# A Mamba, attention and gated feed-forward layer in two passes: two adding transfers, one accumulation and one transposition of the first pass moved one step

## The reference, cut to what matters

```
xc, res = x @ W_in.T                          # 1024 channels each
u     = silu(conv4(xc) + b_conv)
dt, B, C = u @ W_xproj.T                      # 32, 16 and 16 columns
delta = softplus(dt @ W_dt.T + b_dt)
h[t]  = exp(delta[t] * A) * h[t-1] + delta[t] * B[t] * u[t]     # 16 states per channel
y[t]  = sum over the 16 states of h[t] * C[t]
out   = ((y + u * D) * silu(res)) @ W_out.T
x     = layernorm(x + out)
```

## Time and profile before

| what | value |
|---|---|
| runs | 2470.24 and 2456.21 us, median 2463.22 us |
| profiled execution | 2475.47 us, its span 2473.7 us |
| first pass in it | about 1,700 us of the span |
| PE busy, whole span | 2333.5 us (94%) |
| DVE busy, whole span | 1852.8 us (75%) |
| ACT busy, whole span | 1565.1 us (63%) |
| POOL busy, whole span | 1670.3 us (68%) |
| granted clock of TensorE, mean | 0.981 |

### The profile page before, as it was taken

One profiled execution on the slowest core, in us unless ns is written; L12 is line 12 of the kernel. 1 busy time (PEld: TensorE's weight loads), 2 busy tenths in 40 slices (PEclk: granted clock), 3 DMA queues, 4 the chain that ended last, 5 costly groups with the idle time before them and its releaser, 6 DMA issues. The chain is left out here.

```text
span 2473.7 us, 38405 instructions
## 1 busy us (share of the span) xinstructions
PE 2333.5 (94%) x15232; PEld 1392.6 (56%) x15232; DVE 1852.8 (75%) x2166; ACT 1565.1 (63%) x2604; POOL 1670.3 (68%) x909
## 2 busy tenths in 40 slices
PE   8898999999899999999999999898899999999998
PEld 4565666566566666556666655554545554554553
DVE  4998898898899899889889887772474565466363
ACT  3786887878778788777788877762333343443432
POOL 1898899898899889888989888882432333233130
PEclk9999999999999999999999999998899999999999
DMA  6677978877877878797787777866200100000000
GB/s 207 141 154 161 223 156 177 218 169 164 212 163 171 189 191 168 158 225 160 174 216 164 175 185 180 196 148 170 103 1 34 35 18 18 34 18 1 17 18 17
DMA packets 103525, 329.57 MB, mean 133 GB/s; under 512 B 9571, under 2 KB 46819, under 8 KB 72627
## 3 DMA queue, kind: packets, MB, share of 16 engines
q0 software_dynamic: 27648, 201.34, 41.3%
q1 hardware_dynamic: 75699, 125.78, 14.9%
HBM read 107.25 MB, written 18.51 MB: 51 GB/s over the span
## 5 line engine op out<-in xcount | busy, mean ns | idle before, releaser
L1020 POOL TENSOR_TENSOR mamba_ring<-mamba_ring,mamba_c_row 128x1024 f32<-128x1024 f32 x512 | 1277.0, 2655 | 45.1 <-DVE mamba_ring L908 44.6
L908 DVE TENSOR_TENSOR_SCAN mamba_ring<-mamba_ring,ps 128x512 f32<-128x512 f32 x1024 | 1175.0, 1201 | 141.1 <-PE ps L452 135.7
L713 ACT ACTIVATE mamba_ring<-mamba_delta,mamba_a_neg 128x512 f32<-128x512 f32 x1024 | 660.4, 710 | 91.6 <-DMA mamba_ring<-mamba_ring 90.0
L452 PEld LDWEIGHTS ps<-shared,mamba_v_t 64*128 64x128 f32 x8192 | 501.2, 189 | 257.8 <-issue 148.0
L452 PE MATMUL ps<-shared,mamba_v_t 64*128 64x128 f32 x8192 | 583.4, 285 | 62.1 <-DVE mamba_ring L908 61.0
L1029 POOL DMA_DIRECT2D mamba_ring<-mamba_ring x192 | 181.5, 945 | 154.9 <-DMA mamba_ring<-mamba_ring 130.5
L1703 POOL TENSOR_TENSOR xf_pr<-xf_pr,xf_top 128x1232 f32<-128x1232 f32 x32 | 75.0, 2343 | 255.5 <-DVE xf_top L1602 255.5
L418 PE MATMUL ps<-mamba_xt,mamba_wres 128*128 128x512 f32 x512 | 242.1, 616 | 0.0
L361 PE MATMUL ps<-mamba_xt,mamba_wu 128*128 128x512 f32 x464 | 218.5, 614 | 5.4 <-DMA mamba_xt<-x_t 5.4
L882 DVE SCALAR_TENSOR_TENSOR mamba_u<-ps,mamba_wcv,mamba_u 128x511 f32<-128x511 f32 (+2 forms) x192 | 142.2, 741 | 73.7 <-ACT mamba_u L678 71.2
L504 PE MATMUL ps<-mamba_wout,mamba_u 128*128 128x512 f32 x352 | 167.9, 611 | 0.0
(11 more groups left out here) (150 smaller groups left out, 2859.6 us busy)
## 6 DMA issues: line engine op xcount, KB each, us to landing
mamba_ring<-mamba_ring POOLq DMA_DIRECT2D x192, 1024.0 KB, 7.7
mamba_c_row<-c_rows SPq DMA_DIRECT2D x32, 1024.0 KB, 12.1
mamba_wres<-w_res SPq DMA_DIRECT2D x64, 256.0 KB, 6.5
mamba_wu<-w_u SPq DMA_DIRECT2D x58, 256.0 KB, 4.1
x_rows<-x SPq DMA_DIRECT2D x32, 256.0 KB, 7.5
mamba_xt<-x_t SPq DMA_DIRECT2D x7, 1024.0 KB, 10.7
x<-x_rows SPq DMA_DIRECT2D x28, 256.0 KB, 5.3
xf_xn<-x SPq DMA_DIRECT2D x16, 256.0 KB, 7.8
```

The source lines that it names most:

```text
L452: m = nc.tensor.matmul(ps[:, 2 * s + i, tb * P:(tb + 1) * P], v_t[g % 2][i * H:(i + 1) * H, tb * P:(tb + 1) * P], diag_b[i * H:(i + 1) * H ...
L713: a = nc.scalar.activation(ring[:, q % NR, i, :], delta[:, d % EARLY, :], ACT.Exp, scale=a_neg[:, d, 2 * k + i:2 * k + i + 1])
L908: m = nc.vector.tensor_tensor_scan(ring[:, r, i, :], ring[:, r, i, :], both[:, bass.ds(i, T, 2)], 0.0, ALU.mult, ALU.add)
L1020: nc.gpsimd.tensor_tensor(ring[:, q % NR], ring[:, q % NR], c_row[:, 2 * k:2 * k + 2, :], ALU.mult).then_inc(c_done, 1)
```

## The change

Four things of the first pass move, each to a neighbouring place of the same step list.

- POOL issues the second adding transfer of a group after the product of step 5, and no longer after that of step 6.
- POOL issues the third one after the product of step 0 of the next group, and no longer after that of step 1.
- PE sums the last two slots (`state_sum`) in step 5 and no longer in step 6, and transposes y back in step 6 and no longer in step 7. In step 5 the sum now stands behind the order of step 4, ahead of other products of step 5. The `if` lines of `v_transposes` and `state_sum` have changed places so that they stand in the order of k.
- ACT copies the sum out and writes the skip term in step 6 and no longer in step 7, ahead of all else of that step.

The amount of work, its shapes and its data are the same. The first adding transfer stays where it was, after the product of step 3.

```
@@ -557,11 +557,11 @@  PE
-                if k == 6 and g >= 1:
+                if k == 4 and g + 1 < NG:
+                    v_transposes(g + 1)
+                if k == 5 and g >= 1:
                     for e in SUMS:
                         state_sum(g - 1, e)
-                if k == 4 and g + 1 < NG:
-                    v_transposes(g + 1)
@@ -622,7 +622,7 @@  PE
-                if k == 7 and g >= 1:
+                if k == 6 and g >= 1:
                     y_transposes(g - 1)
@@ -1039,9 +1039,9 @@  POOL
-                    if k == 1 and g >= 1:
+                    if k == 0 and g >= 1:
                         merge(g - 1, 2)
-                    if k in (3, 6):
+                    if k in (3, 5):
                         merge(g, k // 4)
```

## The result

The changed kernel took 2577.57 and 2590.41 us, a median of 2584 us against 2463 us before: +121 us, a ratio of 1.048 with a 95% interval of 1.045 to 1.052. I had forecast slower, 2553 us. The profiled execution took 2577.57 us (span 2575.7), 102 us more than the one of before; +90 us had been forecast for that pair. The second pass kept its length: from the last gating of y to the end there are 762.8 us, and 764.4 before.

The account below looks back on a forecast made before the run. POOL, running behind DVE nearly always, was taken to lead. Longer cycle 153, less 5 (second transfers leaving sooner), 38 (spacing) and 20 (waits for scans), gave +90 us on 2463: 2553 us, range 2500 to 2616 us.

Parts of the forecast that it names:

- POOL's longer cycle: First pass, POOL: each group's cycle grows by one product, 2.43 us, +153 us over 63 distances; +90 us after reliefs.
- Relief by spacing: First transfers, issued longer after a third one, share the DMA engines less: 0.6 us per group, -38 us, bounds 0 and -76.
- rival D: Block 7, DVE: no relief comes and `make_diag` stalls in every batch row, 6.8 us each in three more: +173 us; chance 0.06.
- PE's and ACT's moves at nothing: PE's sum and transposition back, ACT's copy and skip term: costed at 0, at most 28 us of PE freed.
- POOL's waits for scans "vanish": POOL's products before DVE's scans: waits vanish as far as POOL always runs behind, -20 us, bounds 0 and -34.8.
- POOL's unrelieved cycle: First pass, POOL: one product more per group with no relief, +153 us, 2616 us, the range's upper end.
- The rival that the Trainium skill's fit stood behind: POOL's first transfer lands within 5.8 us, so no wait arises, or something else leads: -28 us, 2435 us; chance 0.10.

Follow-up runs that it names:

- the half transfer: First adding transfer of each group adds one of its two slots: on POOL's part alone 2430.7 us, 0.987; on the kernel before 2436.3 us, 0.989.

## Why the prediction was right, and where it was not

**POOL's longer cycle: right for POOL's part by itself.** Forecast +90 us; measured alone +86 us, with the distance from one first transfer to the next up by 1.23 us (1.43 forecast). Its steps one by one: the second transfer can't leave before the first has landed (192 landings of 6.9 us or more; the half transfer shows the point, at 4.5 us the cost is gone). In the changed kernel the product reappears between third and first (+2.77 us of distance, 2.43 forecast; the group shown adds waits for scans). The second to third distance keeps its 9.55 us. Relief by spacing was mis-sized: first transfers land 1.06 us sooner on average, and 0.79 in POOL's part alone; forecast 0.6.

**A term left out.** I kept the stalls of DVE's tiles (rival D) out of the sum, on the ground that POOL's standstill opens gaps for them. In the changed kernel the first tile of block 7 takes 4.3 to 8.5 us in all 7 batch rows that make one; before, it took over 6 us in 4 of them and 0.7 us in the other 3; the 14 tiles take 51.8 us in place of 35.3. That is +16.5 us, where D had 20, and +35 us in POOL's part alone. So the agreement of 90 with 86 is in part luck.

**The failed step: PE's and ACT's moves at nothing.** I wrote that the sum "goes up past one set of `b_products`" and costed PE's move at 0, looking only at what the sum waits for. What counts is what waits behind it. Step 5 has another job on PE, and step 6 has none, so the move stacks 2.0 us on a stretch that already held a job, and the scan of step 7 pays: 13.8 us per batch row in the changed kernel, where all distances between scans together gain 14.8. By itself this part costs 4.3%, more than POOL's, with block 7's wait for the third transfer in it. The forecast put its possible effect between 0 and a gain of 28 us; its sign was wrong.

**POOL's waits for scans "vanish": wrong**, 34.8 to 75.0 us, for the same reason: scans that come late behind PE make POOL wait.

**How the two add.** 3.6% and 4.3% alone give 4.8% together, not 7.9%. On top of PE's and ACT's part, POOL's part costs only 0.5% (1.043 to 1.048, with intervals that overlap), so in the changed kernel PE's part accounts for most of the time. The waits show it: in PE's part alone POOL idles 157.8 us for scans, and its longer cycle fits into that. In POOL's part alone ACT's decays wait 161.8 us for transfers; in the changed kernel 6.5 us, so that POOL's lag hardly reaches the scans by this way. What POOL's part changes on top lies in block 7, and the two halves of it nearly cancel. The third transfer comes early enough for the sum: from scan 6 to scan 7 there are 5.85 us and no longer 12.12, and PE's wait for transfers falls from 44.4 to 12.4 us. And DVE's first tile is stalled again: from scan 1 to scan 2 there are 8.60 us and no longer 3.75, and the 14 tiles take 51.8 us and no longer 18.7. This is read from rows; no run held either fixed.

**The clock** was not in the forecast. The changed kernel has 24 stretches at the lower level; with the sum alone there are 22 and with POOL's part alone 13. No experiment held the clock fixed, so its share stays open. The two distances in blocks 1 and 5 grew by 4.9 us per batch row, 34 us over the 7 batch rows that prepare a next one; that is an estimate of the most that the stretches there cost, as PE's waits before them are in it. What the one in block 7 costs is not in it.

**The range** held the time since its upper end had been set by POOL's unrelieved cycle, +153 us; the middle was low by the second cause. That the whole came within 31 us of the forecast is partly luck: the cause that I named costs about as much alone as I said, but in the changed kernel another one sets most of the time, and the two overlap. Of the rivals none came true as a whole. The rival that the Trainium skill's fit stood behind ("DMA: Bandwidth & Descriptors", anatomy of one DMA) did not: these adding transfers of 1 MB never landed in the 4.4 us that it gives.

## What to carry to other kernels

A step that is moved to "sooner" must be asked two things: does what it waits for come sooner too, and what is queued behind it in its new place? Here a transfer could not leave before another had landed, so an engine idled where it used to work, and a job of 2 us joined a stretch of another engine's list that already held one (4.10 us from scan to scan on average, the longest of the eight). Two causes that each fill the same slack don't add: measure each half of a change alone before believing an account that fits the total.

## What the runs showed of the hardware

An adding transfer of 1 MB within SBUF landed after 6.9 us at the least, one of 0.5 MB after 4.5 us. An estimate from these two shortest landings is 2.4 us per half MB, 218 GB/s, and some 2.1 us that don't depend on the size. The Trainium skill's page "DMA: Bandwidth & Descriptors", anatomy of one DMA, gives 2.0 us and 436 GB/s: the fixed part agrees with these runs, and the rate measured here is half of the page's. No run here has such a transfer without the add, so whether the add is the reason is not shown.

A DVE operation with two inputs in SBUF (`make_diag`) took 0.66 us at the shortest and up to 12.2 us when POOL ran product after product (the trace of POOL's part alone):

```profile
L897 DVE TENSOR_TENSOR shared<-mamba_eye,mamba_b_col x22: 657/946/12214, 46.1 to 1535.5; 128x512 f32<-128x512 f32 x22
```

The longest began at 1516.12 and ended at 1528.33. In this time POOL ran four products (about 2.65 us each), one `make_v` and the issue of a transfer without a gap, and the tile was done 0.6 us behind the last of them. The page "SBUF — State Buffer" of the Trainium skill, two separate sides, has the loser blocked for the whole of one instruction; here it was passed over by the next ones as well.
